# Slots stage of a fused attention and soft-MoE layer: slots' inputs turned in 32x32 blocks on VectorE and moved by 16 DMAs, in place of four transposes on TensorE

## The reference, cut

```python
logits   = einsum('bnd,des->bnes', x_n, mu_n)      # B=2, N=2048, D=512, E=16, S=128
dispatch = softmax(logits, axis=1)                 # over the tokens n
slot_in  = einsum('bnd,bnes->besd', x_ln, dispatch)
h        = gelu(einsum('besd,edh->besh', slot_in, W1) + b1)
slot_out = einsum('besh,ehd->besd', h, W2) + b2
```

## Time and profile before

| | us |
|---|---|
| median of 3 runs | 2562.74 (2562.68 to 2563.24) |
| the profiled execution | 2560.52 |
| its span, first to last instruction | 2558.5 |
| TensorE busy | 2469.5 (97%) |
| VectorE busy | 1725.5 (67%) |
| GpSimd busy | 1651.2 (65%) |
| ScalarE busy | 1437.7 (56%) |

### The profile page before, as it was taken

The page is one execution under the profiler, slowest core; times in us unless marked ns, Lnnn a source line. Parts: engine busy times, 40 slices in busy tenths (PEclk is TensorE's granted clock), DMA queues, the critical chain, the costliest instruction groups (busy, mean ns, idle before and its releaser), DMA issues. The chain is left out here.

```text
span 2558.5 us, 39425 instructions
## 1 busy us (share of the span) xinstructions
PE 2469.5 (97%) x13218; PEld 1726.4 (67%) x13218; DVE 1725.5 (67%) x3757; ACT 1437.7 (56%) x2764; POOL 1651.2 (65%) x1699
## 2 busy tenths in 40 slices
PE   8989999999999999997989999998999997999998
PEld 6865555555555555553767888887888886788886
DVE  3338887878787878761886565668565564777776
ACT  3214566666666666664775565567556563454553
POOL 4403868686868777676975766765666766455554
PEclk9978999999999999998989999999999998999999
DMA  7861121212121211101966454567454447574553
GB/s 249 273 190 37 35 62 37 61 40 61 37 65 34 67 46 52 47 22 50 332 236 179 140 166 135 159 200 205 135 165 138 155 152 247 181 231 132 144 154 102
DMA packets 232666, 329.59 MB, mean 129 GB/s; under 512 B 56560, under 2 KB 102672, under 8 KB 228240
## 3 DMA queue, kind: packets, MB, share of 16 engines
q1 hardware_dynamic: 195856, 283.47, 36.3%
q0 software_dynamic: 35968, 43.06, 5.8%
q10 hardware_dynamic: 640, 0.55, 0.1%
HBM read 180.63 MB, written 112.22 MB: 114 GB/s over the span
## 5 line engine op out<-in xcount | busy, mean ns | idle before, releaser
L846 ACT ACTIVATE p_probs<-p_ps_s 128x512 f32<-128x512 f32 (+3 forms) x1280 | 598.0, 540 | 340.6 <-PE p_ps_s L779 331.1
L1424 POOL DMA_DIRECT2D p_eT<-p_ex x1024 | 539.9, 536 | 268.8 <-DVE p_ex L1690 216.9
L877 DVE TENSOR_REDUCE p_parts<-p_ps_m 128x1 f32<-128x512 f32 x768 | 472.4, 682 | 92.8 <-PE p_ps_m L766 92.5
L731 POOL TENSOR_TENSOR p_added<-p_added,p_probs 128x2048 f32<-128x2048 f32 x112 | 513.6, 4586 | 20.6 <-ACT p_probs L846 8.4
L766 PE MATMUL p_ps_m<-k_m,q 96*128 96x512 f32 (+3 forms) x1280 | 476.6, 403 | 7.6 <-PEq L1965 3.5
L779 PE MATMUL p_ps_s<-q,k_e 98*128 98x512 f32 (+3 forms) x1280 | 451.1, 382 | 2.3 <-ACT p_probs L846 2.2
L766 PEld LDWEIGHTS p_ps_m<-k_m,q 96*128 96x128 f32 x1280 | 242.6, 192 | 181.5 <-DVE p_parts L877 89.8
L779 PEld LDWEIGHTS p_ps_s<-q,k_e 98*128 98x128 f32 x1280 | 238.3, 191 | 136.3 <-issue 57.7
L881 DVE CUSTOM_DVE_ANT_0 p_masked<-p_ps_m,p_mask 128x384 f32<-128x384 f32 (+3 forms) x512 | 223.8, 487 | 105.0 <-PE p_ps_m L766 98.1
L798 PE MATMUL p_ps_c<-p_probs,v_e 128*32 128x512 f32 (+3 forms) x2560 | 288.3, 541 | 4.7 <-POOL p_probs L716 4.6
L1824 POOL TENSOR_TENSOR p_acc<-p_acc,logit 128x512 f32<-128x512 f32 x112 | 162.4, 1450 | 152.5 <-ACT logit L1877 149.3
(11 more groups left out here) (190 smaller groups left out, 4791.3 us busy)
## 6 DMA issues: line engine op xcount, KB each, us to landing
logits_t<-logit SPq DMA_DIRECT2D x32, 1024.0 KB, 5.0
p_eT<-p_ex POOLq DMA_DIRECT2D x1024, 32.0 KB, 2.1
logit<-logits_t SPq DMA_DIRECT2D x128, 256.0 KB, 3.5
q<-q_t SPq DMA_DIRECT2D x96, 256.0 KB, 4.6
c_first<-L_ffn_W_dram SPq DMA_DIRECT2D x64, 256.0 KB, 5.7
p_x<-L_attn_x_dram SPq DMA_DIRECT2D x32, 256.0 KB, 5.4
q_t<-p_f_hi SPq DMA_DIRECT2D x32, 256.0 KB, 6.0
q_t<-p_f_lo SPq DMA_DIRECT2D x32, 256.0 KB, 6.1
```

What stands on the lines that cost most here:

```text
L731: pool.tensor_tensor(a[:, :, :], first[:, :, :], probs[s % RING][:, :, :], ALU.add).then_inc(s_add, 1)
L846: act.activation(probs[s % RING][:, h, q0:BLK], ps_s[:, u % ST_BANKS, q0:BLK], ACT.Exp).then_inc(s_exp, 1)
L877: dve.tensor_reduce(to, bank, AX.X, ALU.max).then_inc(s_taken, 1)
L1424: pool.dma_start(eT[r][p * QD:(p + 1) * QD, i, :, :], ex[i * QD:(i + 1) * QD, 2 * r:2 * r + 2, bass.ts(p, P)]).then_inc(s_eT[r], 16)
```

## The change

slot_in stays in `si` on 128 partitions. VectorE transposes each 32x32 block of `si` in place (`turn_slot_in`, first in its list). Then `move_slot_in`, first in SyncE's list, issues 16 DMAs that put 32 partitions of blocks each at their place in `siT_lo`: 32 partitions, four runs of 32 numbers (128 bytes) in each, on both sides, 16 KB a DMA. ScalarE's `slot_in_hi` and VectorE's `slot_in_lo` read `siT_lo` from SBUF rather than PSUM. For the last unit SyncE issues eight of the moves and GpSimd the other eight. The four transposes on TensorE are gone. TensorE's order is now logits(0) to (3), product(0), hidden, product(1), product(2), slot_out, product(3). slot_in_hi stands behind vectors_hi, gelu behind split_hi(2), hidden_lo behind split_lo(2), bias behind split_lo(3).

```diff
@@ -1298,7 +1298,8 @@
         s_id0, s_id = sem("id0"), sem("id")
         s_log, s_cp, s_most, s_ex, s_max, s_neg = (sem(n) for n in ("logits", "copied", "most", "exp", "max", "negated"))
         s_sum, s_rs, s_turn, s_ehi, s_elo, s_prod = (sem(n) for n in ("sum", "inverse", "turned", "e_hi", "e_lo", "product"))
-        s_si, s_sT, s_sThi, s_sTlo = sem("slot_in"), sem("slot_in_t"), sem("slot_in_hi"), sem("slot_in_lo")
+        s_si, s_sT, s_sThi, s_sTlo = sem("slot_in"), sem("slot_in_turned"), sem("slot_in_hi"), sem("slot_in_lo")
+        s_siT, s_last = sem("slot_in_moved"), sem("last_slot_in_moved")
         s_h, s_g, s_hhi, s_hlo, s_o = sem("hidden"), sem("gelu"), sem("h_hi"), sem("h_lo"), sem("slot_out")
         s_add, s_ohi, s_olo = sem("biased"), sem("o_hi"), sem("o_lo")
         s_mt, s_mc, s_mr, s_mrow = sem("most_t"), sem("m_col"), sem("m_row_t"), sem("m_row")
@@ -1347,6 +1348,15 @@
                                          d["xl"][(B - 1 - n // E) * NT + j * TG + p].rearrange("(t a) c -> a t c", a=QD)).then_inc(s_xl[j], 16)
                 return part
 
+            def move_slot_in(n):
+                sp.wait_ge(s_sT, n + 1)
+                if n > 0:
+                    sp.wait_ge(s_h, n)
+                for q in range(NQ if n < UNITS - 1 else NQ // 2):
+                    for a in range(NQ):
+                        sp.dma_start(siT_lo[q * QD:(q + 1) * QD, :, a * QD:(a + 1) * QD].bitcast(F32),
+                                     si[a * QD:(a + 1) * QD, :].rearrange("p (c q j) -> p c q j", q=NQ, j=QD)[:, :, q, :]).then_inc(s_siT, 16)
+
             def first_rows(n):
 
                 if n == 0:
@@ -1402,7 +1412,7 @@
                     for e in range(E):
                         sp.dma_start(kept_xT[:, e, :].bitcast(F32), d["so"][0, 0, :, e, :]).then_inc(s_next, 16)
 
-            walk([(0, load_mu)] + [(0, load_unit_rows(j)) for j in range(JG)]
+            walk([(3, move_slot_in), (0, load_mu)] + [(0, load_unit_rows(j)) for j in range(JG)]
                  + [(1, first_rows), (1, store_logits)] + [(2, load_weights)] + [(1, later_rows)] + [(3, store_out)]
                  + [(1, next_slots), (2, next_logits)])
             sp.wait_ge(s_next, 16 * (E + 5))
@@ -1423,6 +1433,12 @@
                         for i in range(NQ):
                             pool.dma_start(eT[r][p * QD:(p + 1) * QD, i, :, :],
                                            ex[i * QD:(i + 1) * QD, 2 * r:2 * r + 2, bass.ts(p, P)]).then_inc(s_eT[r], 16)
+            pool.wait_ge(s_sT, UNITS)
+            pool.wait_ge(s_h, UNITS - 1)
+            for q in range(NQ // 2, NQ):
+                for a in range(NQ):
+                    pool.dma_start(siT_lo[q * QD:(q + 1) * QD, :, a * QD:(a + 1) * QD].bitcast(F32),
+                                   si[a * QD:(a + 1) * QD, :].rearrange("p (c q j) -> p c q j", q=NQ, j=QD)[:, :, q, :]).then_inc(s_last, 16)
             pool.wait_ge(s_log, 4 * UNITS)
             pool.wait_ge(o_so, 32 * E)
             for e in range(E):
@@ -1464,19 +1480,13 @@
                     mm.then_inc(s_prod, 1)
                 return part
 
-            def slot_in_t(n):
-                pe.wait_ge(s_si, n + 1)
+            def hidden(n):
+                pe.wait_ge(s_wlo, 2 * n + 1)
+                pe.wait_ge(s_sTlo, n + 1)
                 if n > 0:
                     pe.wait_ge(s_add, n)
                     if starts(n):
                         pe.wait_ge(s_mrow, n // E)
-                for c in range(DC):
-                    mm = pe.transpose(ps_e[:, 0, bass.ts(c, P)], si[:, bass.ts(c, P)], ident[:, :])
-                mm.then_inc(s_sT, 1)
-
-            def hidden(n):
-                pe.wait_ge(s_wlo, 2 * n + 1)
-                pe.wait_ge(s_sTlo, n + 1)
                 for c in range(DC):
                     mm = three_passes(pe, ps_e[:, 0, 0:S], w1_hi[:, c, :], w1_lo[:, c, :],
                                       siT_hi[:, c, :], siT_lo[:, c, :], c == 0, c == DC - 1)
@@ -1504,9 +1514,8 @@
                 if starts(n) and n > 0:
                     pe.wait_ge(s_mrow, n // E)
 
-            walk([(1, logits(0)), (3, slot_in_t), (1, logits(1)), (1, logits(2)), (3, hidden),
-                  (1, logits(3)), (3, slot_out), (2, product(0)), (2, product(1)), (2, product(2)), (1, largest_t),
-                  (2, product(3)), (2, largest_rows)])
+            walk([(1, logits(0)), (1, logits(1)), (1, logits(2)), (1, logits(3)), (2, product(0)), (3, hidden),
+                  (2, product(1)), (2, product(2)), (3, slot_out), (1, largest_t), (2, product(3)), (2, largest_rows)])
 
         @block.scalar
         def _(act):
@@ -1568,15 +1577,19 @@
                 act.wait_ge(s_prod, 4 * n + JG)
                 act.wait_ge(s_rs, n + 1)
                 if n > 0:
-                    act.wait_ge(s_sT, n)
+                    act.wait_ge(s_siT, 256 * n)
                     act.wait_ge(s_olo, n)
                 act.activation(si[:, :], ps_s[:, 0, :], ACT.Copy, scale=col[n % 2][:, 11:12]).then_inc(s_si, 1)
 
             def slot_in_hi(n):
-                act.wait_ge(s_sT, n + 1)
+                if n < UNITS - 1:
+                    act.wait_ge(s_siT, 256 * (n + 1))
+                else:
+                    act.wait_ge(s_siT, 256 * n + 128)
+                    act.wait_ge(s_last, 128)
                 if n > 0:
                     act.wait_ge(s_h, n)
-                act.activation(siT_hi[:, :, :], ps_e[:, 0, :], ACT.Copy).then_inc(s_sThi, 1)
+                act.activation(siT_hi[:, :, :], siT_lo[:, :, :].bitcast(F32), ACT.Copy).then_inc(s_sThi, 1)
 
             def gelu(n):
                 act.wait_ge(s_h, n + 1)
@@ -1612,9 +1625,10 @@
                     act.wait_ge(s_mrow, n // E + 1)
                     act.dma_start(d["top"][n // E], m_row[:, :]).then_inc(o_m, 16)
 
-            walk([(3, slot_in), (1, copy(0)), (3, slot_in_hi), (1, copy(1)), (2, split_hi(0)), (2, rows_hi(0, False)),
-                  (1, copy(2)), (3, gelu), (2, rows_hi(1, False)), (2, split_hi(1)), (1, copy(3)), (2, rows_hi(2, False)), (0, vectors_hi), (1, exp(0)), (1, exp(1)),
-                  (2, split_hi(2)), (2, rows_hi(3, False)), (1, exp(2)), (1, exp(3)), (2, split_hi(3)),
+            walk([(3, slot_in), (1, copy(0)), (1, copy(1)), (2, split_hi(0)), (2, rows_hi(0, False)),
+                  (1, copy(2)), (2, rows_hi(1, False)), (2, split_hi(1)), (1, copy(3)), (2, rows_hi(2, False)), (0, vectors_hi), (3, slot_in_hi),
+                  (1, exp(0)), (1, exp(1)),
+                  (2, split_hi(2)), (3, gelu), (2, rows_hi(3, False)), (1, exp(2)), (1, exp(3)), (2, split_hi(3)),
                   (0, unit_rows_hi(0)), (0, unit_rows_hi(1)), (3, out_hi),
                   (0, unit_rows_hi(2)), (0, unit_rows_hi(3))]
                  + [(1, rows_hi(j, True)) for j in range(JG)] + [(2, weights_hi), (2, largest_row)])
@@ -1690,9 +1704,13 @@
                     dve.transpose(ex[:, j, :], ex[:, j, :]).then_inc(s_turn, 1)
                 return part
 
+            def turn_slot_in(n):
+                dve.wait_ge(s_si, n + 1)
+                dve.transpose(si[:, :], si[:, :]).then_inc(s_sT, 1)
+
             def slot_in_lo(n):
                 dve.wait_ge(s_sThi, n + 1)
-                dve.tensor_tensor(siT_lo[:, :, :], ps_e[:, 0, :].rearrange("p (c s) -> p c s", c=DC), siT_hi[:, :, :], ALU.subtract).then_inc(s_sTlo, 1)
+                dve.tensor_tensor(siT_lo[:, :, :], siT_lo[:, :, :].bitcast(F32), siT_hi[:, :, :], ALU.subtract).then_inc(s_sTlo, 1)
 
             def hidden_lo(n):
                 dve.wait_ge(s_hhi, n + 1)
@@ -1720,10 +1738,11 @@
                             dve.wait_ge(s_mr, n // E)
                         dve.tensor_reduce(m_col[:, group(j)], ps_l[:, j, :].rearrange("p (t s) -> p t s", t=TG), AX.X, ALU.max).then_inc(s_mc, 1)
 
-            walk([(3, slot_in_lo), (1, maximum(0)), (1, largest(0)), (1, maximum(1)), (2, split_lo(0)), (1, largest(1)), (2, rows_lo(0, False)),
-                  (1, maximum(2)), (3, hidden_lo), (2, rows_lo(1, False)), (2, split_lo(1)), (1, maximum(3)), (3, bias), (2, rows_lo(2, False)),
-                  (0, vectors_lo), (1, largest(2)), (1, turn(0)), (1, turn(1)), (2, split_lo(2)), (2, rows_lo(3, False)), (1, turn(2)), (1, turn(3)),
-                  (2, split_lo(3)), (0, unit_rows_lo(0)),
+            walk([(3, turn_slot_in), (1, maximum(0)), (1, largest(0)), (1, maximum(1)), (2, split_lo(0)), (1, largest(1)), (2, rows_lo(0, False)),
+                  (1, maximum(2)), (2, rows_lo(1, False)), (2, split_lo(1)), (1, maximum(3)), (2, rows_lo(2, False)),
+                  (0, vectors_lo), (3, slot_in_lo), (1, largest(2)), (1, turn(0)), (1, turn(1)), (2, split_lo(2)), (3, hidden_lo),
+                  (2, rows_lo(3, False)), (1, turn(2)), (1, turn(3)),
+                  (2, split_lo(3)), (3, bias), (0, unit_rows_lo(0)),
```

## The result

The changed kernel takes 2776.7 us (median of 4 runs, 2775.62 to 2781.34), against 2562.7 before: a ratio of 1.0839, 95% interval 1.082 to 1.0857. The profiled execution took 2781.34 us, 220.8 more than the 2560.52 of before. The forecast of 2605 had the sign and the mechanism; the size is outside its range of 2570 to 2690.

A forecast was written before the change was run, and what follows sets the result against it. TensorE's issue was taken to bound the steady steps. Per step -0.44 for transposes and +1.29 stall gave +0.85, over 29 steps +25 us; with +18 at the ends, +43, so 2605 us, range 2570 to 2690 (8 in 10).

The forecast's parts named there:

- Transposes, 0.44 us: TensorE, each step: removing the four transposes was to save 0.44 us, 14 us over 32 units.
- S: Zero point of a step's times: the start of TensorE's first matmul of logits(0); the next S was 24.65 us later before.
- The pitch of the moves, 0.465: SyncE's 16 moves: one issue per 0.465 us, bounds 0.42 to 0.65, the last issued by S+9.1.
- V: Start of vectors_hi on ScalarE, once the slot vectors' load has landed; forecast S+13.15, against S+11.83 when it would like to start.
- rival A: Long pitch on SyncE: 0.65 us an issue, stall 4.3, 2690, or 2750 with the slower clock; chance 0.14.
- The chain from V to the hidden layer: vectors_hi, vectors_lo, then slot_in_lo: TensorE may start hidden at V+1.97, S+15.12, standing 1.29 us a step.
- The floor: VectorE's first free place behind maximum(3): hidden not before S+14.27, so TensorE stands 0.44 us even with DMAs in time.
- The ends, +18: Stage's ends and change of batch: three extra terms, together +18 us, between +8 and +26.
- (c): Change of batch: row loads queue behind the b2 load, which waits for the late bias; about +4 us.
- (a): Last but one step: unit 30's moves queue behind 16 next-stage loads; slot_in(30) to slot_in(31) 31.1 us, before 23.9; +7.
- (b): Last unit, moves split between SyncE and GpSimd: slot_in to slot_in_hi 7.8 us instead of 1.44; +6.4.
- C: Faster rival: VectorE hands over slot_in_lo in time for S+13.83, saving 0.44 us a step; 2553 to 2558; chance 0.07.

## Why the prediction missed

**What bounds the kernel, and the frame of the step**: right. Four transposes more cost their full length, taking them away gave 0.28 of 0.44 us, and the new stall fell on TensorE in full. In the list of waits a larger one stood than the 6.5 us that I named, 8.4 us in three waits for the low half of the exponentials; it lies outside the steady steps too and changes nothing.

**Transposes, 0.44 us**: right as their price (doubled, +0.44). As a gain it is 0.28, once the hidden layer has been moved, because slot_in_lo is still a little late there.

**The turn, done at S+1.6**: it starts at S+1.11 behind weights_lo and the moves start at S+1.84, 0.2 us late. No matter.

**The pitch of the moves, 0.465**: this is the step that failed. It is 0.65 in the median of the bursts, my upper end, and 0.666 in the step shown (10.65 us for 16). I had two rows to choose from, and chose by the number of dimensions: the earlier trace rows had three, as the moves have, and the earlier trace rows more. The runs show that dimensions and the length of the runs are together worth 0.01 us, and that both sides in SBUF are worth 0.17 (0.602 against 0.433). By that property the copy of the earlier trace rows, 0.612 us, was the only near row. With this pitch the moves are late as well: I had them landed before vectors_hi could start, at S+11.2, and with the load out of their way slot_in_hi waited for them in 14 of 14 steps (17.2 us in all).

**Landing**: 1.9 us for the moves where 2.1 was taken, 3.2 for load_mu where 4.1 was. Both are kinder than forecast. V was S+15.84, close to the S+16.1 of rival A: its pitch and its landing erred in opposite directions, so that closeness is luck in part.

**The chain from V to the hidden layer**: right. V+1.97 gives S+17.81; the first matmul of the hidden layer is at S+17.89. The wait, the engine and the tile were those named. No second stall arose before product(3). The floor that I set, a hidden layer not before S+14.27, was reached by no run with the changed kernel's order: with the load ahead of the moves it starts at S+14.92 in the step shown.

**512-byte runs**: the row on landing spoke against this, and the runs bear it out: one run of 512 bytes instead of four of 128 changes neither issue nor landing. The rule of the Trainium skill ("DMA: Bandwidth & Descriptors", Specifications) bound nothing here. The same page, in the section Issuing engines are not separate DMA queues, says that starting transfers from several engines saves only the sequencer's time, which is usually small. Here that time, 10.65 us of a step of 30.94, is what holds the load of the slot vectors up.

**The clock**: in the sum I had none, since a stall of 1.29 us was forecast. The runs agree that this holds for most such stalls: in the kernels with the load first and with the filled gap, idle times up to 1.33 us cost none in 45 of 45 steps (the hidden layer takes 1.29 to 1.40 us), between 1.47 and 2.55 us some do and some don't (1.36 to 2.07), and in the changed kernel from 3.34 us on all 30 do (2.58 to 2.60). Under rival A I put it at 2 us; it is 2.65 (1.26 + 1.39), nineteen matmuls and not nine. The range stopped at 2690, rival A without the clock, so the 2750 that I had worked out for it lay outside. The Trainium skill ("TensorE: Matmul & The Clock Gate", What's actually happening) calls the low clock the default, which activity releases; the filled stall agrees, 1.00 where it was 0.89.

**The ends, +18**: they are some +42. Taking 29 x 6.16 = 179 off 220.8 leaves 42. (c) The three steps at the change of batch grew by 31.2, which is 12.7 more than three ordinary ones (3 x 6.16) where I had 4 without a sum behind it; b2's place alone gave back 12.4. (a) From slot_in(30) to slot_in(31), at 2334.05 and 2369.21, it is 35.2 us and not 31.1: the 16 moves behind the 16 loads took 10.37 and not 7.4. SyncE's queue there in the changed kernel:

```profile
2331.84 9.01 SPq L1413 DMA_DIRECT2D kept_xT<-slot_out  x16
2340.94 10.37 SPq L1357 DMA_DIRECT2D p_siT_lo<-p_si  x16
```

(b) From slot_in to slot_in_hi of the last unit it is 10.1 and not 7.8. SyncE's half goes out 1.5 us after slot_in, at 2370.68, but GpSimd's only 4.4 us after it, at 2373.65. With GpSimd's own loads put ahead of them these moves start 1.7 us after slot_in, and the wait is 7.8 as forecast; why they start so late in the changed kernel the traces don't show. And from there to the stage's end it takes 19.3 us where it took 11.1. I had said that GpSimd's own 16 loads would end about together with the rest, but they go out as late as 2377.98 to 2386.48. With them ahead of the moves the end of the stage follows the last slot_in by 18.9 us and not by 29.4; 2.3 of that are the earlier moves, and 8.2 the loads, as much as this whole excess. The matmuls of the last unit run at 1.2 GHz in the kernel before and in the changed one (granted clock 0.53 and 0.50).

**The rivals.** A, the long pitch, was the case that happened, with 2690 and, with the clock, 2750; my weighing gave it 0.14. What lies between 2750 and 2776.7 is for the most part the ends, +42 where it has 18; each step is 0.4 us longer too. A time like C's can be had, but only with other orders on four engines: it is the kernel with five units on TensorE, 2555.4.

**What followed from one wrong term.** The pitch error is 16 x 0.2 = 3.2 us of issue. With the shorter landing it made V 2.7 us later than forecast and the stall 2.8 us longer (4.12 against 1.29). The clock then added 2.65, so that the step grew by 6.29 and not by 0.85: nearly half of the error is a second price that the first one set off.

## What to carry to other kernels

Price the issue of a transfer by a row with the same memories on both sides; here shape and run length were worth 0.01 us. When a burst of issues is put into an in-order queue, look first at the small load behind it: putting that load ahead was worth 129 us here, while the pattern of the moves was worth 1. Look at the irregular steps too: where no ordinary step got longer, 16 issues whose data nobody used still cost some 28 us at the change of batch and at the end. And if a stall of several microseconds is possible, its price is the stall plus the matmuls behind it at the lower clock, so the range has to reach that case.

## What the runs showed of the hardware

- On SyncE's queue an issue takes 0.60 us for an SBUF to SBUF move of 32 partitions and 0.43 us if the source is in device memory, in the same place of the same kernel. A load from device memory takes 0.59 us right behind the former and 0.43 right behind the latter. GpSimd issues the SBUF to SBUF moves in 0.54 (4.33 us for eight).
- After 3.96 us of idle time TensorE's granted clock is 0.50 for some five microseconds, though it works all through them. After 1.33 us and less the matmuls kept their length at 2.4 GHz in 45 of 45 steps; after 1.55 us the clock once fell to 0.53. Twelve matmuls a step whose result nobody reads make the changed kernel 2% faster for that reason.
